# Recurrence of batch 1: an earlier norm, low parts on the vector engine, and Pool's chunk lows moved

## What is computed

```python
# third: a recurrence over time, per batch and feature
xs = shifted(x)                                   # one token back
k = (x*tmk + xs*(1-tmk)) @ Wk.T + bk
v = (x*tmv + xs*(1-tmv)) @ Wv.T + bv
r = silu(x*tmr + xs*(1-tmr)) @ Wr.T + br
t  = maximum(u + k_t, w)
a  = exp(-w-t)*a + exp(u+k_t-t)*v_t ;  b = exp(-w-t)*b + exp(u+k_t-t)
out = ((a/b) * r) @ Wo.T + bo
# fourth: 32 experts of width 96, the best 4 of each token, and a shared expert of width 704
out = sum_e combine_e * (silu(x@wg_e)*(x@wu_e)) @ wd_e + sigmoid(x@seg)*(silu(x@sg)*(x@su))@sd
```

## Time and profile before

| what | us |
|---|---|
| runs of the kernel, median of 3 (526.77, 526.46, 522.57) | 526.46 |
| the profiled execution, its own time | 521.88 |
| its span, first to last instruction | 519.9 |
| mean clock that PE was granted, of full speed | 0.928 |
| PE busy, share of the span | 83% |

### The profile page before, as it was taken

The page is one execution under the profiler, slowest core; times in us unless marked ns, Lnnn a source line. Parts: engine busy times, 40 slices in busy tenths (PEclk is TensorE's granted clock), DMA queues, the critical chain, the costliest instruction groups (busy, mean ns, idle before and its releaser), DMA issues.

```text
span 519.9 us, 10001 instructions
## 1 busy us (share of the span) xinstructions
PE 432.7 (83%) x3396; PEld 297.6 (57%) x3396; DVE 341.6 (66%) x851; ACT 280.8 (54%) x554; POOL 235.9 (45%) x316
## 2 busy tenths in 40 slices
PE   7987899899998799787987347698889899999654
PEld 2664455454555387676775325487668566666343
DVE  5976687688782758546469956995743555555346
ACT  7645767677776631424855188434432455555302
POOL 7874553456674305102402371337465155555600
PEclk9978999899999999898999667789989999999968
DMA  8345345111110298000000101899622454444182
GB/s 231 112 128 157 79 133 143 37 39 48 31 28 4 84 315 265 1 1 0 1 1 0 31 0 32 230 226 298 204 89 91 101 151 134 135 129 126 53 326 84
DMA packets 51674, 55.63 MB, mean 107 GB/s; under 512 B 10080, under 2 KB 42729, under 8 KB 51624
## 3 DMA queue, kind: packets, MB, share of 16 engines
q1 hardware_dynamic: 47176, 46.26, 32.5%
q0 software_dynamic: 4448, 8.73, 4.9%
HBM read 35.22 MB, written 21.73 MB: 110 GB/s over the span
## 4 chain that ended last, share of the span: by engine, by line
PE 47%; DVE 25%; issue 8%; SPq 7%; ACT 6%; DMA 4%; POOL 2%; POOLq 0%; DVEq 0%; ACTq 0%
PE ps L2470 7%; PE ps L2186 5%; PE ps L2236 5%; PE ps L2165 4%; PE ps L2224 4%; PE ps L2495 4%; PE ps L2226 4%; PE ps L2225 3%; PE ps L2451 3%; DVE st L1032 3%; PE ps L2144 3%; SPq L564 2%; DVE h_lo L1200 2%; SPq L592 2%; DMA max_parts_scratch<-m_cols 2%
## 5 line engine op out<-in xcount | busy, mean ns | idle before, releaser
L1765 ACT ACTIVATE probs<-ps 128x512 f32<-128x512 f32 x160 | 87.0, 598 | 34.7 <-PE ps L2165 33.4
L1133 DVE TENSOR_REDUCE negm<-ps 128x2 f32<-128x1024 f32 (+1 forms) x64 | 67.4, 1081 | 14.6 <-PE ps L2154 14.5
L897 POOL DMA_INDIRECT y_slots_scratch<-yblk,ids x48 | 47.2, 984 | 47.9 <-issue 30.9
L712 POOL TENSOR_TENSOR rstd<-ve,halfneg 128x4 f32<-128x4 f32 x15 | 15.8, 1053 | 82.8 <-DVE ve L1051 27.5
L2186 PE MATMUL ps<-probs,v_all 128*32 128x128 f32 (+3 forms) x512 | 48.3, 452 | 2.1 <-DVE att L1161 1.6
L1801 ACT CAST h_hi<-hf 128x512 fp32r<-128x512 f32 x28 | 17.4, 620 | 60.4 <-DVE hf L1191 60.4
L2165 PE MATMUL ps<-q_ring,k_all 64*128 64x512 f32 (+3 forms) x256 | 40.2, 371 | 11.0 <-DMA q_ring<-max_parts_scratch 5.3
L2144 PE MATMUL ps<-k_all,q_ring 64*128 64x512 f32 (+3 forms) x256 | 46.5, 374 | 2.5 <-DVE negm L1133 1.4
L2165 PEld LDWEIGHTS ps<-q_ring,k_all 64*128 64x128 f32 x256 | 20.8, 186 | 44.4 <-ACT probs L1765 32.0
L1528 DVE COPY xcol<-ps 128x256 f32<-128x256 f32 x48 | 20.4, 424 | 34.9 <-PE ps L2451 34.9
L2470 PE MATMUL ps<-wgu,xcol 128*64 x188 | 40.6, 339 | 0.0
(11 more groups left out here) (367 smaller groups left out, 1349.4 us busy)
## 6 DMA issues: line engine op xcount, KB each, us to landing
x_sorted_scratch<-pad SPq DMA_DIRECT2D x6, 1072.0 KB, 13.0
xblk<-x_sorted_scratch SPq DMA_DIRECT2D x96, 67.0 KB
wgu<-in_moe_w SPq DMA_DIRECT2D x4, 1536.0 KB, 17.8
ycomb<-y_slots_scratch SPq DMA_DIRECT2D x8, 512.0 KB, 6.7
q_ring<-q_parts_scratch SPq DMA_DIRECT2D x60, 64.0 KB
wd<-in_moe_w SPq DMA_DIRECT2D x1, 3072.0 KB, 21.1
sraw<-in_moe_w SPq DMA_DIRECT2D x6, 384.0 KB, 3.3
q_parts_scratch<-qparts SPq DMA_DIRECT2D x4, 512.0 KB, 4.8
```

What stands on the lines that cost most here:

```text
L897: pool.indirect_dma_start(out=y_slots, out_offset=bass.IndirectOffsetOnAxis(ap=ids[:, i:i + 1], axis=0), in_=yblk[:, i % YR, :], in_offset ...
L1133: dve.tensor_reduce(negm[:, par, :, hp, qt], pair_of, AX.X, ALU.max, negate=True).then_inc(s1_read, 1)
L1765: act.activation(probs[:, par, u, :], ps[:, col_unit(g, u), :], ACT.Exp)\
```

## The change

DVE: the residual (first operation of a quotient) becomes a function of its own; `out_stats(1,1)` moves between the residual and the rest of quotient(0,1); `in_apply(1,1)` is replaced by `in_shift(1,1)` and `in_half(1,1)`, which stand ahead of `out_stats(2,0)` and `out_apply(2,0)`; the mix lows of batch 1 are done by DVE, each behind its mixes; `out_stats(2,0)` stands behind the first mixes and low, `out_apply(2,0)` behind the second ones, `in_shift(2,0)` behind mixes(1,2). ACT: two of the four row tiles of (1,1) are written by `apply_rows`; the PSUM reads of the keys become `read_keys`, ahead of the table load; chunk_high(4) moves behind the first shared unit and chunk_high(5) behind the second. Pool: power 8 ahead of the second low of batch 0; chunk lows 0 and 1 wait for the rows of (1,1) and stand ahead of power 10; chunk lows 2 to 4 wait for the mask of batch 0; chunk low 5 stands between scatter(0) and power 13.

```diff
+        SHIFTS = [(1, 1), (2, 0), (2, 1)]
@@ Pool
             for q in range(3):
-                mix_low(0, q)
+                mix_low(pool, 0, q)
             wkv_low(pool, 0, 0)
+            power(8)
             wkv_low(pool, 0, 1)
-            power(8)
             power(9)
+            pool.wait_ge(rows_ready, 4 * TPB)
+            chunk_low(0)
+            chunk_low(1)
             power(10)
-            chunk_low(0)
             power(11)
-            mix_low(1, 0)
-            mix_low(1, 1)
-            mix_low(1, 2)
-            chunk_low(1)
+            pool.wait_ge(mask_ready, 1)
             chunk_low(2)
-            for c in range(3, SHARED):
-                chunk_low(c)
+            chunk_low(3)
+            chunk_low(4)
             pool.wait_ge(s_sorted, 6 * 16)
             power(12)
             scatter(0)
+            chunk_low(5)
             power(13)
@@ DVE
-            def in_half(b):
-
-                dve.wait_ge(nmr_ready, b + 1)
+            def in_half(part, b):
+
+                new = (xb, xa)[part % 2]
+                dve.wait_ge(nmr_ready, SHIFTS.index((part, b)) + 1)
...
+            residual(0, 0)
             quotient(0, 0)
+            residual(0, 1)
+            out_stats(1, 1)
             quotient(0, 1)
-            out_stats(1, 1)
             out_apply(1, 1)
-            out_stats(2, 0)
-            in_apply(1, 1)
-            out_apply(2, 0)
+            in_shift(1, 1)
+            in_half(1, 1)
...
             mixes(1, 0)
+            mix_low(dve, 1, 0)
+            out_stats(2, 0)
+            mixes(1, 1)
+            mix_low(dve, 1, 1)
+            out_apply(2, 0)
+            mixes(1, 2)
             in_shift(2, 0)
-            mixes(1, 1)
-            mixes(1, 2)
+            mix_low(dve, 1, 2)
             scan(1, 0)
             scan(1, 1)
+            residual(1, 0)
             quotient(1, 0)
             split_low(3, 0)
             wkv_low(dve, 1, 0)
+            residual(1, 1)
             quotient(1, 1)
@@ ACT
             chunk_high(1)
+            apply_rows(1, 1, TPB // 2)
             columns(1)
             mixes(1, 0)
             mixes(1, 1)
             mixes(1, 2)
+            read_keys()
             act.preload_act_table_set(LOG_AND_EXP)
             exponents()
-            apply_rows(0, 0)
+            apply_rows(2, 0, 0)
...
             shift(1, 1)
-            chunk_high(4)
             wkv_high(1, 1)
...
             shared_unit(0)
+            chunk_high(4)
+            shared_unit(1)
             chunk_high(5)
-            shared_unit(1)
             shift(2, 0)
             shared_unit(2)
-            apply_rows(1, TPB // 2)
+            apply_rows(2, 1, TPB // 2)
```

More of the change, by code:

```diff
@@ L460, in col_unit, with mix_low @@
             return 4 + (2 * CU * g + u) % 3
+        def mix_low(eng, b, q):
+            for k in range(DC):
+                eng.wait_ge(mix_hi, (3 * b + q) * DC + k + 1)
+                eng.tensor_tensor(m_lo[:, q, k, :], mixed[:, (3 * b + q) % 2, k, :],
+                                  m_hi[:, q, k, :].bitcast(F32), ALU.subtract)\
+                    .then_inc(mix_lo, 1)
         def wkv_low(eng, b, m):
@@ L844, in _ @@
             pool.memset(onesE[:, :], 1.0).then_inc(s_const2, 1)
[L846 to L852, removed]
             def chunk_low(c):
@@ L1242, in scan, with residual @@
                                                   0.0, ALU.mult, ALU.add))
-            def quotient(b, m):
+            def residual(b, m):
                 dve.wait_ge(inv_ready, 2 * b + m + 1)
@@ L1250, in quotient @@
                     decay[:, m, :], den[:, m, :], -1.0, gain[:, m, :], ALU.mult, ALU.mult))
+            def quotient(b, m):
                 chain.step(dve.tensor_tensor(num[:, m, :], num[:, m, :], gain[:, m, :],
@@ L1503, in _ @@
             in_shift(2, 1)
-            in_half(1)
+            in_half(2, 1)
             shared_low(2)
@@ L1826, in mixes, with read_keys @@
                     act.copy(m_hi[:, q, k, :], mixed[:, at, k, :]).then_inc(mix_hi, 1)
+            def read_keys():
+                for m in range(DC):
+                    act.wait_ge(proj_k, 2 + m + 1)
+                    act.wait_ge(wkv_done, m + 1)
+                    act.activation(decay[:, m, :], ps[:, 6 + m, :], ACT.Relu,
+                                   bias=ubw[:, m:m + 1]).then_inc(k_read, 1)
+                    act.activation(gain[:, m, :], ps[:, 6 + m, :], ACT.Relu,
+                                   bias=wub[:, m:m + 1], scale=-1.0).then_inc(k_read, 1)
             def copy_logits(b):
@@ L1842, in exponents @@
             def exponents():
-                for m in range(DC):
-                    act.wait_ge(proj_k, 2 + m + 1)
-                    act.wait_ge(wkv_done, m + 1)
-                    act.activation(decay[:, m, :], ps[:, 6 + m, :], ACT.Relu,
-                                   bias=ubw[:, m:m + 1]).then_inc(k_read, 1)
-                    act.activation(gain[:, m, :], ps[:, 6 + m, :], ACT.Relu,
-                                   bias=wub[:, m:m + 1], scale=-1.0).then_inc(k_read, 1)
                 for m in range(DC):
@@ L1919, in route, with apply_rows @@
                 act.activation(wtop[:, h, :], wtop[:, h, :], ACT.Exp).then_inc(route_exp, 1)
-            def apply_rows(b, first):
-                act.wait_ge(nmr_ready, b + 1)
+            def apply_rows(part, b, first):
+                new = (xb, xa)[part % 2]
+                act.wait_ge(nmr_ready, SHIFTS.index((part, b)) + 1)
                 for t in range(b * TPB + first, (b + 1) * TPB):
-                    act.activation(rows[:, t, 0:D], xb[:, t, :], ACT.Identity,
+                    act.activation(rows[:, t, 0:D], new[:, t, :], ACT.Identity,
                                    bias=nmr[:, t:t + 1], scale=rstd[:, t:t + 1])\
```

2 lines of the change are left out of this document (1 added, 1 removed).

## The result

| | before | after |
|---|---|---|
| median of 20 runs, us | 526.26 | 522.30 |
| lowest and highest | 522.13 to 530.08 | 517.81 to 524.63 |
| the profiled execution, its own time | 521.88 | 524.37 |
| its span | 519.9 | 522.6 |

A forecast was written before the change was run, and what follows sets the result against it. DVE, partly held by Pool, was taken to bound the changed stretch, then PE, nearly gap-free behind 352.7 us. Leads 1.2 + 1.5 + 1.5, less 0.6 and 1.1, gave 2.5 us: 524.0 us, range 520.5 to 527.5.

The forecast's parts named there:

- Step A: Norm of batch 1 started earlier on DVE: its rows ready at 290.8 instead of 295.1, a lead of 4.3 us.
- Step B: Batch 1's three mixes: key lead of 5.7 us, all spent in DVE's queue before the SiLU load near 306.1.
- Step C: Keys read ahead of ACT's second table load: PE's values 1.3 us earlier, first value scan 1.2 us earlier.
- Step D: Pool's chunk lows behind the mask: `num` and `topf` gain 1.5 each, one hold returns; lead 4.2 at mask, 3.6 at `h_lo(1)`.
- Step E: Chunk low 5 ahead of the last power delays `h_lo(2)`: lead 2.5 us at PE's transposes, kept gap-free to the end.
- The surviving lead: Rival: the 5.7 us key lead survives DVE's queue, 5.5 to 6 us gained in all, 520.7; chance 0.14.
- The slower one: Rival: chunk lows 2, 3 and 4 each hold a DVE operation beside route_places(0) for 1.5 us, 527.0; chance 0.10.
- SP's later weight loads: Expert weight loads end about 380 instead of 372, hidden by some 20 us because blocks begin after 400.

The follow-up runs named there:

- e1: Changed kernel with key reads behind the table load again and Pool's chunk lows not waiting for the mask, leaving the earlier norm and DVE low parts; ratio 0.9980.
- e7: Changed kernel with mixes(1,2) on DVE ahead of out_apply(2,0); ratio to before 0.9894.
- e8: Changed kernel with the six mix lows of batch 1 back on Pool; ratio to before 0.9922.
- e11: Kernel before with only the six mix lows of batch 1 moved to DVE, the norm left in place; ratio 1.0006.
- e2: Kernel before with only the four PSUM reads of the keys put ahead of the table load; ratio 0.9934.
- e4: Changed kernel with only the key reads put back behind the table load; ratio to before 0.9928.
- e5: Changed kernel without Pool's wait for the mask of batch 0 ahead of chunk low 2; ratio to before 0.9924.
- e6: Changed kernel with chunk low 5 behind power 13 instead of ahead of it; ratio to before 0.9934.
- e3: Kernel before with only the Pool part: chunk lows 2 to 4 behind the mask, chunk casts 4 and 5 later, chunk low 5 ahead of power 13; ratio 0.9986.
- e9: Kernel before, unchanged, traced a second time; SiLU load at position 30.96 against 29.38 in the first trace.
- e12: Changed kernel with batch 1's norm back behind the whole second quotient, out_stats(2,0) and out_apply(2,0) ahead of the mixes, power 10 ahead of chunk low 0; ratio to before 0.9917.
- e10: Changed kernel with mixes(1,2) ahead of out_apply(2,0), chunk low 5 behind power 13, and ACT's SiLU table loaded between mixes(1,0) and mixes(1,1); ratio to before 0.9853.

## Why the prediction was right, and where it was not

**Step A** gave the rows a lead of 4.3; they have 4.8 (13.56 against 18.33).

**Step B** gave the keys 5.7 and had all of it spent before the SiLU load, at 306.1. The keys have 6.2, and the load is at 28.92, 305.7 on the clock of before. The mechanism is shown by e1 (nothing at the mask) and e7 (3.5 of it back when the queue is changed). What the step missed is on the other side of the comparison: it took the load of before at 306.12 as a fixed mark. In three of four traces of that kernel's list it lies 1.1 later, since Pool's low part holds `mixed`. I had `mixed` at 301.48 among the odd pieces and didn't ask about the next pair, which by the same rule hangs on a tie. So the low parts on DVE don't only cost 3.9 us of queue, as the step put it: they take that hold away (e8 and e11).

**Step C**, 1.3: it is 1.41 (e2) and 1.43 (e4). The first scan came at 38.08 against 39.95, 1.9 for the 1.2 forecast: the other half microsecond is from step B. The Trainium skill, ScalarE: Activation LUTs (What ACT_TABLE_LOAD costs), puts a switch at 2.7; the traces don't agree, and they decide.

**Step D**, 1.5 + 1.5 with one hold in return: `num` gave 1.5 and `topf` 1.6; the mask's lead of 4.2 is 4.55. Behind the mask there are two holds, 1.4 and 0.8, where before had one of 1.5. `h_lo(1)` has 3.8 for the 3.6 forecast. But why `h_lo(1)` has less lead than the mask, the step had wrong. It cut 0.6 because PE would become the limit, with shared_up(1) at 340.8, a lead of 3.1; its own terms give 339.6 (337.5 - 4.2, and 6.3 on top), and measured is 339.4 on the clock of before, a lead of 4.5. PE was no limit. The 0.7 that is lost from mask to `h_lo(1)` is the holds, 1.4 + 0.8 now and 1.5 before; in e5, with one hold of 1.5, this stretch takes 14.91, as before (14.89). Right in size, by another cause. The gain of the step in all is smaller than it looks, since without the wait for the mask the holds only lie elsewhere (e5). And of the mask's lead 0.5 went to PE's clock: DVE waited 0.71 for the logits products, which ran at the lower level (e4), against 0.22 before.

**Step E** put the transposes of (3,1) 2.5 us ahead, and they are: 81.69 against 79.18. But its reason failed in this trace, and that the number came out is luck. PE's clock had fallen and the stretch took 1.3 longer, and `h_lo(2)` was ready before PE wanted it. Where the clock stays high (e4, e5, e8), PE waits 0.85 for it and the stretch takes 1.1 longer than before, as the step has it: the two causes happen to cost nearly the same. The step's last sentence, that PE is free of gaps from there and takes the lead to the end, is wrong for both kernels. The next place where the clock shows is further on, where PE stands until the block table of batch 0 (`blkB`) is made. The timeline of PE in the kernel before, the transposes behind that wait, the first of the twelve `shared_up` products behind them and the first down product:

```profile
379.48 0.38 PE L2441 MATMUL ps<-ident,blkB 128*1 128x128 f32 x2 [3.17 <-DVE blkB L1466]
379.79 0.50 PE L2224 MATMUL ps<-cols_hi,schunks 128*128 128x512 f32 x1
...
384.23 0.28 PE L2236 MATMUL ps<-schunk,h_hi 128*128 128x256 f32 x1
```

and the same in the kernel after:

```profile
380.80 0.58 PE L2459 MATMUL ps<-ident,blkB 128*1 128x128 f32 x2 [3.14 <-DVE blkB L1471]
381.31 0.80 PE L2242 MATMUL ps<-cols_hi,schunks 128*128 128x512 f32 x1
...
386.56 0.28 PE L2254 MATMUL ps<-schunk,h_hi 128*128 128x256 f32 x1
```

The lead at the transposes is 2.65 (102.74 against 100.09), and PE idled as long in both, 3.17 and 3.14. But the twelve products took 4.44 (384.23 - 379.79) before and 5.25 after (386.56 - 381.31), so that 1.6 is left at the down product and to the last `h_lo`. The same twelve took 5.20 to 5.29 in e4, e6 and e8, 3.99 to 4.45 in e2, e3, e5, e7, e9, e11 and e12, and 2.85 and 2.86 in e1 and e10. The granted clock over them was 0.50 in after, 0.62 in before and 1.00 in e1. So that PE's clock decides here is shown; why it stays low for longer in some kernels isn't, and it stays open.

**Sum.** 2.5 was forecast and 3.5 measured, inside the range and the interval. The missing microsecond is the size of the hold that the trace of before didn't show; by positions to the last `h_lo` the lead is 1.6 against the first trace and 3.0 against the second. That the hold is the whole difference isn't shown, for the time's interval is wider than it. Nor do the times divide the gain among the parts: e2, the key reads alone on the kernel before, is as fast as the whole change (0.9934 against 0.9933), and e4, the change without them, is too (0.9928).

**The rivals.** The surviving lead (5.5 to 6) isn't what this change does, but it is what e10 does, beyond it: 7.7. The slower one, three holds beside route_places, got two holds, the shorter for 0.8. SP's later weight loads cost nothing that the trace of after shows: the blocks began behind the dense units as before.

## What to carry to other kernels

A lead at the head of a stage is worth what is left of it behind the fullest in-order queue: list what the moved work pushes, and in front of which operation another engine is waiting, before counting the lead; work that nobody awaits belongs beside the awaited engine's own work (e7), and a table load where that engine idles (e10). And one trace is one draw: where two engines ask for the same thing within hundredths of a microsecond, look at a second trace of the unchanged kernel before taking a row as its time. When times differ by less than their spread, compare positions from a common instruction instead of spans, and then check that nothing behind the last position gives the lead back (`xblk` here).

## What the hardware showed that I had not expected

- A Pool tensor operation beside it holds DVE until it ends not only in the forms seen before (`num`, `mixed`, a cast) but also in a scan of 32 elements (1.64 for 0.23) and a copy of 16 (0.98 for 0.17); readings from PSUM beside Pool kept their time (`st` 1.42 beside a power in before, `xb` 1.65 beside two low parts in e8). Moving the Pool operation by one place moves the hold to whichever such row is next (e5, e6).
- Which of the two goes first can differ between executions of the same list: 3.07 for Pool's two lows in one trace, 2.52 in three.
- PE's clock fell in 5 of 6 waits of 2.38 us and more in front of the second shared down product, and in none of 8 of 1.72 and less. In front of the routing logits, behind waits of 2.48 to 2.56, it was low in two traces (after, e1) and full in four (e4, e5, e8, e10). Waits that differ by hundredths of a microsecond can be followed by either level.
